# Record scatters of a graph kernel: eleven tiles per step beside the pair experts instead of eight, and none beside the slice attention

## The chip, the cores and the metric

The kernel runs on one core of a Trainium2 chip, in a single launch. The metric is the device time in microseconds (us), and the median of three runs stands for the kernel. TensorE is called PE here, VectorE DVE, ScalarE ACT, GpSimd POOL and SyncE SP; SPq and POOLq are the queues from which SP and POOL issue transfers.

## The reference

Four layers, each a graph network and a feed-forward block, over 3125 nodes of 256 values and a graph of 53125 edges (src, dst, a 64-value attribute and a type for each edge). Between the blocks stand a residual and a layer norm:

```
x = x + L0_gnn(ln(x), src, dst)              # batch norm and two GIN convolutions
x = x + L0_ffn(ln(x))                        # slice attention
x = x + L1_gnn(ln(x), src, dst)              # graph attention
x = x + L1_ffn(ln(x))                        # 8 experts, the best two for each node
x = x + L2_gnn(ln(x), src, dst, edge_attr)   # edge network: the only one that reads edge_attr
...                                          # one expert, relations, deep experts
```

The slice attention projects every node, takes a softmax over 64 slices for each of 8 heads, sums the nodes into slice tokens, lets the tokens attend to each other and gives the result back to the nodes. L1_ffn is, for the two experts that a node picks, `gelu((xn * g + b) @ W1 + b1) @ W2 + b2`, with hidden width 1024. L2_gnn needs for each edge its source node, destination node and attribute, and sums the messages by source node.

## The kernel before

Nodes lie in NT = 25 tiles of 128 rows, edges in ET = 416 tiles of 128. The stages of `build` run one after the other: constants, sort_slots (twice), place_edges, gin, slice_attention, graph_attention, expert_pair, edge_update, one_expert, relations, deep_experts. A stage ends with a barrier over all engines. Within a stage each engine has its own program, and they meet in semaphores.

**The records.** edge_update reads a table `rec2` in DRAM, in which the edges stand sorted by source. A record is 68 floats (272 bytes): 64 of the attribute, the other node's number, the row within the tile and two zeros. The table is filled earlier, from POOL, beside other stages: for each tile of 128 edges one indirect DMA ("scatter", L554) writes 128 records to the rows that m.record names. A group is SG = 8 tiles. For a group, SP loads the attributes (`load_group`, L532: 256 KB in pieces of 256 bytes), and POOL copies the two numbers beside them (L547, L549), waits for the load (`arrived`) and issues the scatters (`send_groups`); before a buffer is loaded again SP waits for its scatters (`sent`). The 52 groups are spread over three stages: PLACED = 8 beside place_edges, EARLY - PLACED = 12 beside the slice attention's first big loop, with two buffers in m.XN ("normed" in the profile), and 32 beside the loop of expert_pair, with four buffers in m.AF ("sums").

**The slice attention's loop** (L1104 to L1236) is written out for all 25 tiles, in five rounds of five. Per tile PE runs 4 matmuls of scores (L1193) and 2 for their bias (L1195), whose end is `scored`, 4 for the values (L1199), whose end is `fxed`, and, one tile later, 8 that sum the tokens (L1183; `summed`). DVE takes the maximum as soon as `scored` comes (L1223), subtracts it (L1226), and after ACT's Exp (L1161) sums and divides (L1230 to L1234). ACT copies the values out once `fxed` comes (L1163), keeps the weights (L1151) and stages the next tile (L1147). Each f32 matmul in the code is two in the profile, so the profile counts 18 matmuls and 18 weight loads per tile. POOL has nothing else to do in this stage than the records, and SP after its three first loads neither.

**The pair experts' loop** (L1924 to L2081) takes W = 32 steps of 256 rows, one expert's weights to each. It is a runtime loop whose body holds four steps (`pipeline`: each engine runs a prologue, then the loop, then the last steps written out). Per step PE turns the rows (L2007, 4 matmuls), runs the first layer of the next step (L2018, 32 matmuls, a signal `made` after every 4) and the second layer of this one (L2029, 32 matmuls, `done`). ACT runs 8 Gelus (L2045) on what `made` gives, DVE shapes the turned rows (L2063) and adds the bias (L2071). SP's queue holds, per step, in this order: rows four steps ahead (L1968), w1 of three ahead (1 MB, L1973), w2 of two ahead (1 MB, L1978; waits for `done`), the store (L1982; waits for DVE) and the record group four ahead (L532):

```
            def load_records(d, u, r):
                if not isinstance(d, int) or d >= RING:
                    sp.wait_ge(sent[u], r * (16 * SG))
                load_group(sp, a["edge_attr_64"], records, d + EARLY, u, arrived)

            pipeline(sp, R, (4, load_rows), (3, load_w1), (2, load_w2), (0, store), (4, load_records), total=W)
```

So four groups are loaded ahead of the loop, and from then on one for each step that PE, DVE and SP have finished. POOL's own program (`send_groups`) is written out.

Of the kernel before, what the change touches and what calls it, by code (L numbers as in the profile page):

```python
# [25 lines left out]
P = 128  # L26
# [6 lines left out]
ET = -(-E // P)  # L33
EA = 64
# [5 lines left out]
SG = 8  # L40
# [8 lines left out]
RING = 4  # L49
PLACED = 8  # L50
EARLY = 20
EPS = 1e-5
# [376 lines left out]
def place_edges(nc, m, attr):  # L429

    HALF = NP // 2
    R = SG
    with Stage(nc) as st:
# [31 lines left out]
        @block.gpsimd  # L465
        def _(pool):
            pool.wait_ge(m.rec_blanked, 16 * -(-WP // (BLANK // 4)))
            pool.wait_ge(m.rows_blanked, 16 * ((ROWS + 2 * P) // (P * 6)))
            send_groups(nc, pool, m, records, range(PLACED), arrived, sent, filled)

        @block.sync
        def _(sp):
            for g in range(PLACED):
                if g >= RING:
                    sp.wait_ge(sent[g % RING], g // RING * 16 * SG)
                load_group(sp, attr, records, g, g % RING, arrived)
            for u in range(RING):
                sp.wait_ge(sent[u], len(range(u, PLACED, RING)) * 16 * SG)
# [50 lines left out]

def load_group(sp, attr, records, g, u, arrived):  # L530

    sp.dma_start(records[:, u * SG:(u + 1) * SG, 0:EA], attr.rearrange("(t p) c -> p t c", p=P)[:, bass.ds(g * SG, SG), :]  # L532
                 ).then_inc(arrived[u], 16)


def send_groups(nc, pool, m, records, groups, arrived, sent, filled):

    RING = len(sent)

    nc.gpsimd.memset(records[:, :, EA + 2:EA + 4], 0.0).then_inc(filled, 1)  # L540
    pool.wait_ge(filled, 1)
    for n, g in enumerate(groups):
        u, r = n % RING, n // RING
        mine, group = slice(u * SG, (u + 1) * SG), slice(g * SG, (g + 1) * SG)
        if r:
            pool.wait_ge(sent[u], r * 16 * SG)
        nc.gpsimd.tensor_copy(records[:, mine, EA], m.oth_e[:, group]).then_inc(filled, 1)  # L547
        pool.wait_ge(filled, 2 * n + 2)
        nc.gpsimd.tensor_copy(records[:, mine, EA + 1], m.lo_e[:, group]).then_inc(filled, 1)  # L549
        pool.wait_ge(filled, 2 * n + 3)  # L550
        pool.wait_ge(arrived[u], r * 16 + 16)
        for k in range(SG):
            t = g * SG + k
            nc.gpsimd.indirect_dma_start(m.rec2, bass.IndirectOffsetOnAxis(ap=m.record[:, t:t + 1], axis=0),  # L554
                                         records[:, u * SG + k, :], None).then_inc(sent[u], 16)

# [464 lines left out]
def slice_attention(nc, m, a):  # L1021
# [84 lines left out]
    with Stage(nc) as st:  # L1106
        filled = st.sem("filled")
        arrived, sent = st.sems("arrived", 2), st.sems("sent", 2)
        records = view(xn, 5280, 2 * SG, EA + 4)
        names = ("loaded", "staged", "scored", "read", "centred", "expd", "weighted", "fxed", "fxcopied", "summed",  # L1110
# [10 lines left out]
        @block.sync  # L1121
        def _(sp):
            sp.dma_start(b_fx, a["L0_ffn_b_fx"].unsqueeze(0).to_broadcast([P, HW])).then_inc(loaded, 16)
            sp.dma_start(w_out, a["L0_ffn_W_out"].rearrange("(r p) d -> p r d", p=P)).then_inc(loaded, 16)
            sp.dma_start(b_out, a["L0_ffn_b_out"].unsqueeze(0).to_broadcast([P, D])).then_inc(loaded, 16)
            sp.wait_ge(loaded, 48)
            for n in range(EARLY - PLACED):
                if n >= 2:
                    sp.wait_ge(sent[n % 2], n // 2 * 16 * SG)
                load_group(sp, a["edge_attr_64"], records, PLACED + n, n % 2, arrived)  # L1130
            for u in range(2):
                sp.wait_ge(sent[u], (EARLY - PLACED) // 2 * 16 * SG)

        @block.gpsimd
        def _(pool):
            for s in range(U):
                ins = nc.gpsimd.memset(fx[:, s, :, FW - 1], 1.0)
            ins.then_inc(oned, 1)
            send_groups(nc, pool, m, records, range(PLACED, EARLY), arrived, sent, filled)

# [781 lines left out]
def expert_pair(nc, m, a):  # L1922
# [11 lines left out]
    with Stage(nc) as st:  # L1934
        names = ("turned", "shaped", "made", "active", "done", "ready", "smalls")
        turned, shaped, made, active, done, ready, smalls = (st.sem(s) for s in names)
        R = RING
        filled = st.sem("filled")
        arrived, sent = st.sems("arrived", RING), st.sems("sent", RING)
        records = view(m.AF, 0, RING * SG, EA + 4)  # L1940
        assert EARLY + W == ET // SG
        camex, came1, came2, stored = (st.sems(s, R) for s in ("camex", "came1", "came2", "stored"))
# [16 lines left out]
        def _(sp):  # L1959
# [24 lines left out]
            def load_records(d, u, r):  # L1984
                if not isinstance(d, int) or d >= RING:
                    sp.wait_ge(sent[u], r * (16 * SG))
                load_group(sp, a["edge_attr_64"], records, d + EARLY, u, arrived)

            pipeline(sp, R, (4, load_rows), (3, load_w1), (2, load_w2), (0, store), (4, load_records), total=W)
            for u in range(R):  # L1990
                sp.wait_ge(stored[u], 16 * (W // R + (1 if u > 1 else 0)))
                sp.wait_ge(sent[u], 16 * SG * (W // R))

        @block.gpsimd
        def _(pool):
            send_groups(nc, pool, m, records, range(EARLY, ET // SG), arrived, sent, filled)

# [1086 lines left out]
```

## Time and profile before

| what | value |
|---|---|
| median of three runs | 7234.84 us (7220.34 to 7235.94) |
| the profiled execution's own time | 7225.76 us |
| its span (first to last instruction) | 7224.1 us |
| busy: PE, PEld, DVE, ACT, POOL | 70%, 45%, 46%, 23%, 47% |
| mean granted TensorE clock | 0.819 |
| DMA packets from POOL's queue, share of 16 engines | 17.4% |

PE is the matmul side of TensorE and PEld its weight loads. Every time is from one profiled execution, counted from the span's start. In the order of time, an entry in square brackets is the idle time ahead of the instruction and what the profile takes for its end; "issue" is a wait for nothing that the profile shows, and a DMA named there can be one that merely came last. PEclk is the granted clock of TensorE as a share of full speed: 1.00 is 2.4 GHz, 0.50 is 1.2 GHz, and values between mix stretches of the two.

### The profile page before, as it was taken

The numbers are of one execution on the slowest core, as the hardware profiler recorded it, in microseconds if no ns is written. First come the engines' busy times: TensorE is split into PE (matmuls) and PEld (weight loads), VectorE is DVE, ScalarE is ACT, GpSimd is POOL, SyncE is SP. The second block draws the span as 40 slices with busy tenths as digits, with TensorE's granted clock in tenths as the row PEclk, the third lists the DMA queues.
The fourth block names the chain that finished last, engine by engine and source line by source line (L and its number), as shares of the span: only waits on it lengthen the run. The fifth ranks groups of instructions, "written<-read, shape, count | busy, mean of one in ns | idle before, by whom it ended". The sixth has DMA issues, their size and how long they took to land. (4 is left out here: it accounts for less than half of the span.)

```text
span 7224.1 us, 73624 instructions
## 1 busy us (share of the span) xinstructions
PE 5038.9 (70%) x20207; PEld 3266.0 (45%) x20208; DVE 3353.9 (46%) x7945; ACT 1675.0 (23%) x4060; POOL 3374.7 (47%) x3515
## 2 busy tenths in 40 slices
PE   5946766676638588867774499389998459576545
PEld 1214444444415233345553388378885234343334
DVE  5953334333515466666667011456665442343412
ACT  2930002000212367731112122133333111000111
POOL 4026772666250266657770555266660120666322
PEclk6968888777869689977777699699999779788877
DMA  4013332333110000023330577233340134333245
GB/s 178 2 54 91 91 91 58 89 91 91 32 48 1 22 2 2 2 70 90 91 90 9 160 220 213 69 101 103 106 99 16 52 96 146 90 91 91 51 144 170
DMA packets 405755, 597.99 MB, mean 83 GB/s; under 512 B 131359, under 2 KB 305759, under 8 KB 405279
## 3 DMA queue, kind: packets, MB, share of 16 engines
q0 software_dynamic: 144992, 337.62, 17.4%
q1 hardware_dynamic: 257200, 252.99, 11.3%
q8 instruction: 153, 2.51, 0.1%
q10 hardware_dynamic: 3216, 3.28, 0.1%
q14 instruction: 194, 1.59, 0.1%
HBM read 472.47 MB, written 121.17 MB: 82 GB/s over the span
## 5 line engine op out<-in xcount | busy, mean ns | idle before, releaser
L711 PE MATMUL ps<-zerow,zerob 128*128 128x440 bf16 x2640 | 812.3, 394 | 655.1 <-issue 399.4
L699 POOL DMA_INDIRECT wide<-table,src x880 | 882.0, 1002 | 792.7 <-ACTq L95 404.4
L741 DVE TENSOR_TENSOR sums<-sums,ps 128x256 f32 x1320 | 555.3, 421 | 1237.3 <-PE ps L714 490.4
L714 PE MATMUL ps<-wide 128*128 128x256 f32 x2640 | 906.8, 428 | 20.1 <-DMA wide<-table,src 7.9
L711 PEld LDWEIGHTS ps<-zerow,zerob 128*128 128x128 bf16 x2640 | 245.3, 104 | 999.7 <-issue 569.8
L714 PEld LDWEIGHTS ps<-wide 128*128 128x128 f32 x2640 | 568.8, 219 | 195.0 <-issue 60.6
L699 POOL DMA_INDIRECT wide<-table_rel,rel x440 | 437.8, 995 | 417.0 <-ACTq L95 218.5
L1642 POOL DMA_INDIRECT wide<-table_gat,src x440 | 472.5, 1074 | 218.4 <-issue 121.9
L2255 POOL DMA_INDIRECT work<-table,work x440 | 442.6, 1006 | 262.5 <-PE ps L2292 129.4
L1530 POOL DMA_INDIRECT work<-table_max,src x440 | 438.4, 996 | 198.9 <-issue 128.5
L1549 PE MATMUL ps<-wide,work 128*128 128x512 f32 x880 | 491.0, 642 | 0.0
L1673 PE MATMUL ps<-wide,work 128*128 128x260 f32 x880 | 323.9, 510 | 122.5 <-issue 62.5
L1511 ACT ACTIVATE wide<-ident,work 128x128 f32<-128x128 f32 x1320 | 397.9, 386 | 23.5 <-DMA work<-table_max,src 19.0
L649 ACT COPY work<-sums 128x256 f32<-128x256 f32 x100 | 31.7, 401 | 1359.7 <-PEq L653 1359.6
L660 PE MATMUL ps<-ident,work 128*128 128x128 f32 x650 | 112.2, 332 | 331.8 <-ACT work L649 331.8
L554 POOL DMA_INDIRECT rec<-sums,record x256 | 248.2, 970 | 200.4 <-DMA sums<-in_edge_attr 127.6
L1578 DVE TENSOR_REDUCE work<-ps 128x16 f32<-128x2048 f32 x110 | 251.8, 2290 | 190.9 <-DMA normed<-in_edge_attr 127.6
L2283 PE MATMUL ps<-wide 128*128 x880 | 272.1, 392 | 45.3 <-DVE work L2321 34.4
L1673 PEld LDWEIGHTS ps<-wide,work 128*128 128x128 f32 x880 | 190.8, 243 | 206.3 <-issue 139.3
L1547 PE MATMUL ps<-identb,work 128*128 128x512 bf16 x440 | 180.4, 410 | 148.6 <-issue 108.2
L521 PE MATMUL ps<-wide 128*128 128x441 f16 x832 | 229.1, 365 | 69.5 <-ACT wide L462 48.0
L1744 DVE TENSOR_TENSOR sums<-sums,ps 128x260 f32 x440 | 186.6, 424 | 175.9 <-DMA work<-table_max,src 97.3
(446 smaller groups left out, 9246.1 us busy)
## 6 DMA issues: line engine op xcount, KB each, us to landing
wide<-in_L_ffn_W SPq DMA_DIRECT2D x64, 1024.0 KB
wide<-in_L_ffn_expert_w SPq DMA_DIRECT2D x90, 256.0 KB
table_rel<-wide SPq DMA_DIRECT2D x20, 1024.0 KB
work<-rows_in SPq DMA_DIRECT2D x62, 256.0 KB
rows_out<-work SPq DMA_DIRECT2D x62, 256.0 KB
work<-rec SPq DMA_DIRECT2D x110, 136.0 KB
rec<-work SPq DMA_DIRECT2D x27, 544.0 KB, 16.4
wide<-table,src POOLq DMA_INDIRECT x880
```

Of the source, the lines that this page charges most:

```text
L699: nc.gpsimd.indirect_dma_start(rows[:, w % RT, :], None, table, bass.IndirectOffsetOnAxis(ap=index[:, w:w + 1], axis=0)).then_inc(gathered ...
L711: nc.tensor.matmul(m.PS[:, w % (2 * Q), 0:WT], m.zerob[:, 0:P], m.zerow[:, 0:WT], start=True, stop=True)
L714: nc.tensor.matmul(m.PS[:, w % (2 * Q), 0:D], S[:, w % RT, :], rows[:, w % RT, :], start=True, stop=True).then_inc(summed, 1)
L741: v.tensor_tensor(at, at, m.PS[:, s, 0:D], ALU.add).then_inc(added, 1)
L1511: nc.scalar.mul(diag[:, k * Q + s, h, :], m.ident[:], rows[:, u * Q + s, h:h + 1])
L1530: nc.gpsimd.indirect_dma_start(rows[:, q, :], None, m.table_max, bass.IndirectOffsetOnAxis(ap=m.src1[:, w:w + 1], axis=0)).then_inc(gather ...
L1549: mm = nc.tensor.matmul(at, S[:, k * Q + s, :], diag[:, k * Q + s].rearrange("p h e -> p (h e)"), start=False, stop=True)
L1578: v.reduce_max(top[:, half * Q:(half + 1) * Q, :], m.PS[:, half * Q:(half + 1) * Q, :].rearrange("p s (h e) -> p s h e", h=H), AX).then_in ...
L1642: nc.gpsimd.indirect_dma_start(rows[:, q, :], None, m.table_gat, bass.IndirectOffsetOnAxis(ap=m.src1[:, w:w + 1], axis=0)).then_inc(gather ...
L1673: te.matmul(m.PS[:, 4 + s, 0:RW], S[:, u * Q + s, :], rows[:, u * Q + s, :], start=True, stop=True).then_inc(summed, 1)
L2255: nc.gpsimd.indirect_dma_start(rows[:, k, 0:D], None, m.table, bass.IndirectOffsetOnAxis(ap=idx[:, u * Q + s:u * Q + s + 1], axis=0)).then ...
L2283: te.matmul(at, ST[:, k, :], tile_at(by_src, tiles[s]), start=True, stop=False)
```

## The change

The 12 groups beside the slice attention go; their 96 tiles are sent beside the pair experts, where a group grows from SG = 8 tiles to LG = (416 - 64)/32 = 11. The number of groups there stays 32, one per step, and so does the number of buffers, four. A load is 352 KB instead of 256 KB. `load_group` and `send_groups` take the first tile and the group's size as arguments; place_edges passes 8 and does what it did before.

```diff
 def slice_attention: the loop's stage
-        records = view(xn, 5280, 2 * SG, EA + 4)
             sp.wait_ge(loaded, 48)
-            for n in range(EARLY - PLACED):
-                if n >= 2:
-                    sp.wait_ge(sent[n % 2], n // 2 * 16 * SG)
-                load_group(sp, a["edge_attr_64"], records, PLACED + n, n % 2, arrived)
-            for u in range(2):
-                sp.wait_ge(sent[u], (EARLY - PLACED) // 2 * 16 * SG)
...
             ins.then_inc(oned, 1)
-            send_groups(nc, pool, m, records, range(PLACED, EARLY), arrived, sent, filled)
...
 def expert_pair
-        records = view(m.AF, 0, RING * SG, EA + 4)
-        assert EARLY + W == ET // SG
+        LG = (ET - PLACED * SG) // W
+        records = view(m.AF, 0, RING * LG, EA + 4)
+        assert PLACED * SG + W * LG == ET
...
             def load_records(d, u, r):
                 if not isinstance(d, int) or d >= RING:
-                    sp.wait_ge(sent[u], r * (16 * SG))
-                load_group(sp, a["edge_attr_64"], records, d + EARLY, u, arrived)
+                    sp.wait_ge(sent[u], r * (16 * LG))
+                load_group(sp, a["edge_attr_64"], records, d * LG + PLACED * SG, LG, u, arrived)
...
-                sp.wait_ge(sent[u], 16 * SG * (W // R))
+                sp.wait_ge(sent[u], 16 * LG * (W // R))
...
-            send_groups(nc, pool, m, records, range(EARLY, ET // SG), arrived, sent, filled)
+            send_groups(nc, pool, m, records, range(PLACED * SG, ET, LG), LG, arrived, sent, filled)
```

## Rows read from the trace of the kernel before

**Rows 1.** Line L554: count, min/median/max in ns, first and last start.
```profile
L554 POOL DMA_INDIRECT rec<-sums,record x256: 963/968/989, 4050.8 to 4505.0; - x128
L554 POOL DMA_INDIRECT rec<-normed,record x96: 963/968/1233, 2019.7 to 2148.5; - x96
L554 POOL DMA_INDIRECT rec<-work,record x64: 963/968/1187, 97.6 to 182.8; - x64
```
**Rows 2.** ACT in order of time: Exp starts, slice attention (start, us, engine).
```profile
2022.31 0.63 ACT L1161 ACTIVATE work<-work 128x512 f32<-128x512 f32 x1 [10.35 <-DVEq L1228]
...
2174.80 0.63 ACT L1161 ACTIVATE work<-work 128x512 f32<-128x512 f32 x1 [4.43 <-DVEq L1228]
...
2234.14 0.63 ACT L1161 ACTIVATE work<-work 128x512 f32<-128x512 f32 x1 [4.42 <-DVEq L1228]
...
2255.55 0.63 ACT L1161 ACTIVATE work<-work 128x512 f32<-128x512 f32 x1 [3.96 <-DVEq L1228]
```
**Rows 3.** Windows, slice attention: stretch, us, five engines busy (instructions), PEclk, DMA share, GB/s.
```profile
2040.00:2155.00 115.00, 33.90 (x81) 15.26 (x79) 12.96 (x24) 8.15 (x16) 82.42 (x101) 0.65 0.17 45
2174.80:2204.47 29.67, 28.20 (x91) 13.25 (x90) 15.96 (x30) 9.73 (x21) 0.00 (x0) 1.00 0.00 0
```
**Rows 4.** In order of time, slice attention: PE's two signals and their readers.
```profile
2040.95 1.12 PE L1195 MATMUL ps<-sums,ones 1*128 1x512 f32 x2
2042.00 1.98 PE L1199 MATMUL ps<-sums,work 128*128 128x512 f32 x4
...
2056.08 0.69 DVE L1223 TENSOR_REDUCE normed<-ps 128x8 f32<-128x512 f32 x1 [10.74 <-DMA wide<-table,src]
...
2061.75 0.59 ACT L1163 COPY work<-ps 128x512 f32<-128x512 f32 x1 [3.43 <-DMA wide<-table,src]
```
**Rows 5.** POOL in order of time: first scatter of a group, slice attention.
```profile
2052.42 0.98 POOL L554 DMA_INDIRECT rec<-normed,record  x1 [0.51 <-issue]
```
**Rows 6.** Windows of place_edges, beside scatters and after them.
```profile
120.00:180.00 60.00, 14.53 (x33) 2.17 (x32) 9.27 (x32) 10.64 (x16) 45.21 (x55) 0.50 0.14 39
205.00:225.00 20.00, 19.26 (x74) 4.69 (x74) 19.36 (x74) 20.00 (x37) 0.00 (x0) 1.00 0.01 1
```
**Rows 7.** Windows of the pair experts: the opening burst, the running loop.
```profile
4069.00:4096.00 27.00, 11.55 (x21) 5.41 (x20) 1.00 (x2) 1.68 (x4) 18.70 (x25) 0.59 0.36 116
...
4101.00:4500.00 399.00, 399.00 (x1905) 351.31 (x1904) 47.32 (x84) 93.76 (x230) 223.40 (x274) 1.00 0.73 221
```
**Rows 8.** DVE in order of time: two ends of a step, 27 steps apart.
```profile
4116.53 0.69 DVE L2071 TENSOR_TENSOR work<-ps,work 128x512 f32<-128x512 f32 x1 [12.07 <-PE ps L2029]
...
4501.35 0.69 DVE L2071 TENSOR_TENSOR work<-ps,work 128x512 f32<-128x512 f32 x1 [12.13 <-PE ps L2029]
```
**Rows 9.** POOL in order of time, pair experts: first and last scatter, next burst's first.
```profile
4239.37 0.98 POOL L554 DMA_INDIRECT rec<-sums,record  x1 [3.25 <-DMA sums<-in_edge_attr]
...
4248.29 0.97 POOL L554 DMA_INDIRECT rec<-sums,record  x1 [0.30 <-issue]
...
4253.83 0.98 POOL L554 DMA_INDIRECT rec<-sums,record  x1 [4.10 <-DMA sums<-in_edge_attr]
```
**Rows 10.** In order of time, same step: SP's queue and ACT's first instruction.
```profile
4246.39 0.01 SPq L1982 DMA_DIRECT2D rows_out<-work  x1
...
4247.82 0.01 SPq L532 DMA_DIRECT2D sums<-in_edge_attr  x1
...
4250.88 1.28 ACT L2045 ACT_TABLE_LOAD   x1 [11.08 <-PE ps L2018]
```
**Rows 11.** PE in order of time, opening of the pair experts.
```profile
4069.33 0.38 PE L2018 MATMUL ps<-work,wide 128*128 128x256 f32 x1 [0.29 <-issue]
...
4096.21 5.90 PE L2029 MATMUL ps<-wide 128*128 128x256 f32 x15 [0.82 <-issue]
```
**Rows 12.** DMA by queue, 2016 to 2155: packets, MB, share of 16 engines.
```profile
q8 instruction: 1, 0.02, 0.0%
q14 instruction: 1, 0.01, 0.0%
```

More of the change, by code:

```diff
@@ L50 @@
 PLACED = 8
-EARLY = 20
 EPS = 1e-5
@@ L468, in _ @@
             pool.wait_ge(m.rows_blanked, 16 * ((ROWS + 2 * P) // (P * 6)))
-            send_groups(nc, pool, m, records, range(PLACED), arrived, sent, filled)
+            send_groups(nc, pool, m, records, range(0, PLACED * SG, SG), SG, arrived, sent, filled)
         @block.sync
@@ L475, in _ @@
                     sp.wait_ge(sent[g % RING], g // RING * 16 * SG)
-                load_group(sp, attr, records, g, g % RING, arrived)
+                load_group(sp, attr, records, g * SG, SG, g % RING, arrived)
             for u in range(RING):
@@ L527, in _, with load_group, send_groups @@
             mm.then_inc(placed, 1)
[L530 to L536, printed above, removed]
+def load_group(sp, attr, records, first, size, u, arrived):
+    sp.dma_start(records[:, u * size:(u + 1) * size, 0:EA],
+                 attr.rearrange("(t p) c -> p t c", p=P)[:, bass.ds(first, size), :]).then_inc(arrived[u], 16)
+def send_groups(nc, pool, m, records, firsts, size, arrived, sent, filled):
     RING = len(sent)
@@ L541, in send_groups @@
     pool.wait_ge(filled, 1)
-    for n, g in enumerate(groups):
+    for n, first in enumerate(firsts):
         u, r = n % RING, n // RING
-        mine, group = slice(u * SG, (u + 1) * SG), slice(g * SG, (g + 1) * SG)
+        mine, group = slice(u * size, (u + 1) * size), slice(first, first + size)
         if r:
-            pool.wait_ge(sent[u], r * 16 * SG)
+            pool.wait_ge(sent[u], r * 16 * size)
         nc.gpsimd.tensor_copy(records[:, mine, EA], m.oth_e[:, group]).then_inc(filled, 1)
@@ L551, in send_groups @@
         pool.wait_ge(arrived[u], r * 16 + 16)
-        for k in range(SG):
-            t = g * SG + k
+        for k in range(size):
+            t = first + k
             nc.gpsimd.indirect_dma_start(m.rec2, bass.IndirectOffsetOnAxis(ap=m.record[:, t:t + 1], axis=0),
-                                         records[:, u * SG + k, :], None).then_inc(sent[u], 16)
+                                         records[:, u * size + k, :], None).then_inc(sent[u], 16)
 def blank_records(nc, pool, m, buf, blanked, stored):
@@ L1106, in slice_attention @@
     with Stage(nc) as st:
-        filled = st.sem("filled")
-        arrived, sent = st.sems("arrived", 2), st.sems("sent", 2)
-        records = view(xn, 5280, 2 * SG, EA + 4)
         names = ("loaded", "staged", "scored", "read", "centred", "expd", "weighted", "fxed", "fxcopied", "summed",
```

## The prediction

> **What bounds the kernel now.** I read the page first (no engine is busy for more than 70% of the span, so stages have to be read one by one), then the scatters by line, then the two stretches that the change touches, engine by engine in order of time, then both stretches in windows. The line view of L554 gives 416 scatters of 0.968 us: 64 in place_edges, 96 in the slice attention, 256 in the pair experts [rows 1]. The 96 run from 2019.7 to 2149.5.
>
> The slice attention's loop should be paced by DVE and ACT at one round of five tiles per 29.67 us: that is its pace once the scatters are over ((2234.14 - 2174.80)/2), with the granted clock at 1.00, the 2.4 GHz level [rows 2, 3]. The first Exp (L1161) starts at 2022.3; four rounds later, and 21.41 into the last one (2255.55 - 2234.14), would be 2162.4. The last Exp is at 2255.55 [rows 2]. While scatters run, PE gets 81 matmuls into 115 us, where it later gets 91 into 29.67, and its granted clock is 0.65 [rows 3]. No DMA is short: the DMA share is 0.17 there.
>
> What is late is PE's word. PE has run L1195 of one tile by 2042.1, and DVE, which waits for nothing else, reads that bank at 2056.1; PE ends L1199 at 2044.0 and ACT copies it at 2061.8 [rows 4]. The two lie 5.7 us apart, with 4 matmuls and 4 weight loads between them: 0.71 us per PE instruction. I call that choking. The breaks between groups of eight scatters do not lift it: two copies of 0.20 and a wait of 0.51, about 0.98 without a scatter [rows 5]; it goes on until the last scatter. place_edges shows the same: 33 matmuls in 60 us beside scatters, at the 1.2 GHz level, 74 in 20 us after them [rows 6].
>
> The pair experts' loop is bound by PE: 100% busy over 399 us at clock 1.00, 1905 matmuls and 1904 loads (9.55 instructions per us) [rows 7], and the step is (4501.35 - 4116.53)/27 = 14.25 us [rows 8]. Beside it POOL sends 8 scatters, 9.9 us from the first start (4239.37) to the last end (4249.26), then waits for SP's next load, and starts again at 4253.83: 4.6 us of rest [rows 9]. Choking is there too, late in each burst: SP's queue, which needs no PE for it, goes from its store to its record load in 1.43 us, and ACT gets the first signal of L2018, due about 4246.7, at 4250.9, 1.6 after the last scatter [rows 10]. It begins some 6.5 us into a burst and is lifted about 1.4 after it, and it costs nothing, because PE can run on with signals outstanding and the rest comes every step. In the stage's opening burst (32 scatters in a row from 4050.80, 42.5 us) it isn't hidden: PE stops at 4069.3, 18.5 us into it, does 21 matmuls in 27 us, and is free at 4096.2 [rows 1, 7, 11].
>
> **The change part by part.**
>
> Removed: 96 scatters, 24 POOL copies and 12 loads of 256 KB beside the slice attention. POOL's own time there is on no path; what comes back is the choking: 2255.55 - 2162.4 = **-93 us**. Bounds: -93 if all the lateness is the scatters', and -87 if what passes between the last scatter (2149.5) and DVE's next tile (some 6 us later) has another cause.
>
> Moved: the same 96 scatters to the pair experts, 11 in a group and 352 KB in a load. Copies and loads fall from 32+12 groups to 32 (24 POOL copies of 0.20 and 12 issues are saved, on no path). DMA: a group of eight with its load takes 0.17 of 10.87 us, so three more tiles take 0.7 us per step where the share is 0.73 [rows 3, 7]; not a bound.
>
> Opening burst: four groups of 11 are 4 x (11 x 1.273 + 0.69) - 0.98 = 57.8 us instead of 42.5, and the first, larger load lands about 1.5 later. PE is freed 17 us later and has done some 11 more matmul pairs by then (2.5 us of work): **+14 us**. Bounds 0 and +17.
>
> Steady loop: 11 scatters last 13.7 us; with copies and wait a group takes 14.69 us of POOL, over the step of 14.25. So POOL no longer rests by itself. If nothing choked, the step would be POOL's: 28 x 0.44 = +12 us, the lower bound. But a break of 0.98 doesn't lift the choking [rows 5]. I place PE's stop at 14.5 us into a burst: 9.9 us never stop it, 18.5 did, with some 65 instructions outstanding, and at 9.55 - 1.35 per us these are reached 8 us after the onset at 6.5. Then:
> - Two bursts in a row (28.4 us): PE stands from 14.5 to 29.8, 15.3 us, does 21 instructions (2.2 us of work) and loses 13.1. PE's "done" sits in the choke, so SP issues no further load until 29.8; its queue takes 1.5 and the landing 6 to 7 (4247.82 to 4253.83 is 6.0 for 256 KB [rows 9, 10]), so POOL starts again at about 38.
> - PE's step then ends about 6 us into the next burst, SP's load goes out already choked, lands 16.5 after the burst's start, and this burst stays single. Then the phase is early again and two join.
> - Three groups in 38 + 16.5 = 54.5 us by POOL; by PE 3 x 14.25 + 13.1 = 55.9, and up to 58.5 with the low clock after a stand (15 matmuls in 5.90 us [rows 11], 3.3 at full clock). That is 18.2 to 19.5 per step; I take 18.5: 28 x 4.25 = **+119 us**. Upper bound, if every pair of groups joins (38 us for two): 28 x 4.75 plus nine wakes of 2.6 = +156.
>
> Added waits: none new. SP's wait on sent[u] before a load stands ahead of its rows, w1, w2 and store; the group it asks for was loaded four turns earlier and is sent by then, since POOL has at most two groups before it.
>
> Sum: -93 + 14 + 119 = +40. On the profiled run's own 7225.76 that is 7266; the median of the runs is 9 above it. I take 7272, near the upper of the two (7275).
>
> **A rule beside the rows.** In the slice window the trace holds a single packet of the one instruction queue and one of the other [rows 12], and from 4200 to 4300 the answer lists none. The Trainium skill (Runtime: NRT & Kernel Launch, Instruction fetch mechanics) says that engines stream code in 16 KiB blocks over a DMA queue of their own, in sequence, and that only code outside the loaded window must be fetched. By it, written-out code could starve beside scatters while a loop that is loaded could not. That result is rival A. Against it stand SP and ACT, which are choked inside the loop in each burst [rows 10].
>
> **The rivals.**
>
> A, faster: the code supply of written-out stages is what scatters starve. Place: the slice attention and the opening of the experts, not the running loop. For it: all long stands (slice attention, place_edges, opening) are in written-out code or a loop's first pass. Then -93 + 14 + 12 = -67: 7168. It decides if PE is not stopped by bursts over 14.5 us within the loop. Chance 0.20.
>
> B, faster by less: choking as I say, but the system settles with every burst single, the landing late by its own choke, the break 2 us, step near 16: -93 + 14 + 28 x 1.75 = -30: 7205. For it: SP's lateness does postpone the load. Against it: PE's step end moves earlier in the burst each time that the load comes late. Chance 0.13.
>
> C, same: between B and mine, step near 17: -93 + 14 + 77 = -2: 7233. Chance 0.12.
>
> D, the moved work is hidden and the slice attention gains nothing (PE's signals late for another reason): 7234 + 26 = 7261. The end of the lateness with the last scatter speaks against it. Chance 0.03; it is within my range.
>
> Mine, slower, 0.52 (7272, its own range 7250 to 7320; past that, if most groups join).
>
> **How the numbers follow.** Slower by over 0.2% (which is about what a measurement of this kernel can tell): 0.55. Within it: 0.13. Faster: 0.32, A and B less their edges. The range reaches down to A with its bounds and up to the upper bound of the steady loop: 7158 to 7325.
>
> **What the profile after would show.** Exp's first to last in the slice attention 140 us (was 233), no L554 there, clock near 1. In the experts: 44 scatters in a row at the start, PE free 14 us later. In the loop: breaks of 0.98 between some bursts and over 8 us after others, PE busy 75 to 80% instead of 100, L2071's distance alternating between 14 and some 28 us. If it is regular at 14.7, A is right; at 16, B. I am wrong above all if 0.98 us of break is enough for a looping PE, or if PE's store of outstanding signals is larger than 65.

## The result and the profile after

The changed kernel takes 7319.22 us (median of 4 runs, 7308.93 to 7326.91), the kernel before 7231.72 in the runs beside it: a ratio of 1.0135, 95% interval [1.012, 1.015], slower by some 88 us between the medians, beyond doubt (the two medians alone give 1.0121; the ratio and its interval are taken over all runs). The forecast was 7272, slower by 40. The side was right and the size was not. The profiled execution has a span of 7325.1 us, 101 above that of before.

The slice attention did what was forecast. The time-ordered view of ACT, the Exp (now L1153), answering to [rows 2]:

```profile
2022.25 0.63 ACT L1153 ACTIVATE work<-work 128x512 f32<-128x512 f32 x1 [10.35 <-DVEq L1220]
...
2162.35 0.63 ACT L1153 ACTIVATE work<-work 128x512 f32<-128x512 f32 x1 [3.95 <-DVEq L1220]
```

First to last is 140.1 us where it was 233.2: -93. The windows answer to [rows 3] and [rows 7] (slice attention, opening burst, 28 steps of the pair experts; columns as there):

```profile
2040.00:2155.00 115.00, 109.12 (x347) 50.82 (x345) 61.35 (x115) 37.31 (x77) 0.00 (x0) 1.00 0.00 1
```

```profile
3975.00:4018.00 43.00, 11.74 (x26) 6.23 (x26) 0.99 (x2) 1.68 (x4) 30.84 (x37) 0.58 0.29 89
4025.51:4601.97 576.46, 478.22 (x1904) 375.73 (x1903) 47.34 (x85) 99.99 (x230) 309.20 (x362) 0.86 0.53 162
```

In the slice attention PE now gets 347 matmuls into the same 115 us that held 81. In the opening it does 26 matmuls in 43 us, and in the loop the same 1904 matmuls and 1903 loads that took 399 us at 100% busy take 576.5 at 83%, at a granted clock of 0.86 in place of 1.00. The DMA share falls (0.53): the transfers wait too.

A burst is a group's scatters, sent one after the other; a joined pair is two bursts with so short a break that PE stays held through the second. One joined pair, engine by engine. POOL first (answers to [rows 9]): first and last scatter of the pair's first burst, first and last of its second burst, then the first scatters of the next pair's two bursts.

```profile
4193.58 0.98 POOL L553 DMA_INDIRECT rec<-sums,record  x1 [13.81 <-DMA sums<-in_edge_attr]
...
4206.31 0.96 POOL L553 DMA_INDIRECT rec<-sums,record  x1 [0.30 <-issue]
...
4208.55 0.98 POOL L553 DMA_INDIRECT rec<-sums,record  x1 [0.80 <-DMA sums<-in_edge_attr]
...
4221.27 0.97 POOL L553 DMA_INDIRECT rec<-sums,record  x1 [0.30 <-issue]
...
4236.55 0.98 POOL L553 DMA_INDIRECT rec<-sums,record  x1 [13.83 <-DMA sums<-in_edge_attr]
...
4251.46 0.98 POOL L553 DMA_INDIRECT rec<-sums,record  x1 [0.74 <-issue]
```

PE in the same stretch (answers to [rows 11]):

```profile
4206.25 1.67 PE L2022 MATMUL ps<-wide 128*128 128x256 f32 x7
4208.52 0.38 PE L2022 MATMUL ps<-wide 128*128 128x256 f32 x1 [0.60 <-issue]
4209.99 0.38 PE L2022 MATMUL ps<-wide 128*128 128x256 f32 x1 [1.09 <-issue]
...
4221.38 0.59 PE L2022 MATMUL ps<-wide 128*128 128x256 f32 x1 [1.54 <-issue]
4223.47 3.90 PE L2022 MATMUL ps<-wide 128*128 128x256 f32 x7 [1.51 <-issue]
4227.17 0.85 PE L2000 MATMUL ps<-ident,work 128*128 128x128 f32 x4
```

DVE's end of a step (L2064; answers to [rows 8]), and SP's store and record load (answers to [rows 10]):

```profile
4025.51 0.69 DVE L2064 TENSOR_TENSOR work<-ps,work 128x512 f32<-128x512 f32 x1 [39.78 <-PE ps L2022]
...
4199.23 0.69 DVE L2064 TENSOR_TENSOR work<-ps,work 128x512 f32<-128x512 f32 x1 [14.05 <-PE ps L2022]
...
4227.54 0.69 DVE L2064 TENSOR_TENSOR work<-ps,work 128x512 f32<-128x512 f32 x1 [26.23 <-PE ps L2022]
...
4601.97 0.69 DVE L2064 TENSOR_TENSOR work<-ps,work 128x512 f32<-128x512 f32 x1 [24.20 <-PE ps L2022]
```

```profile
4202.07 0.01 SPq L531 DMA_DIRECT2D sums<-in_edge_attr  x1
...
4228.40 0.40 SPq L1975 DMA_DIRECT2D rows_out<-work  x1
4229.01 0.37 SPq L531 DMA_DIRECT2D sums<-in_edge_attr  x1
```

Read together: the step ends 5.65 us into the burst (4199.23). SP's load goes out at 4202.07 and is down by 4208.55, 15.0 us into the burst, so the second burst follows almost at once. PE works without a break up to 4207.92 (14.3 us in) and comes free at 4223.47, 29.9 us in, after a stand of 15.6 in which it starts 18 matmuls (32 take 7.07 us at full pace). Up to there it is the forecast. But at that moment PE still owes the step 7 matmuls, and they take 3.90 us, since the granted clock is 0.50 there (the 1.2 GHz level). Only at 4227.54 does DVE get its bank, SP loads at 4229.01, and POOL starts at 4236.55, 43.0 us after the pair's start. The step ends 5.5 us into this burst as well, and the next pair joins too. From 4190 to 4240 the DMA view lists no packet of either instruction queue.

### The profile page after: what moved, and what is told of

Same layout as the page of the kernel before. It is cut to its first block and busy times, and to the rows that moved or that the text cites. A ratio compares the mean times of both kernels' runs of the same rounds, so it can differ in the third digit from the quotient of the medians.

```text
span 7325.1 us, 73574 instructions
## 1 busy us (share of the span) xinstructions
PE 5117.0 (70%) x20207; PEld 3287.4 (45%) x20208; DVE 3356.8 (46%) x7945; ACT 1681.2 (23%) x4060; POOL 3362.6 (46%) x3490
## 5 line engine op out<-in xcount | busy, mean ns | idle before, releaser
L713 PE MATMUL ps<-wide 128*128 128x256 f32 x2640 | 909.2, 429 | 20.2 <-DMA wide<-table,src 8.4
L713 PEld LDWEIGHTS ps<-wide 128*128 128x128 f32 x2640 | 570.4, 219 | 195.3 <-issue 62.7
L553 POOL DMA_INDIRECT rec<-sums,record x352 | 340.5, 967 | 294.6 <-DMA sums<-in_edge_attr 185.9
L2022 PE MATMUL ps<-wide 128*128 128x256 f32 x1024 | 295.8, 423 | 114.1 <-issue 111.4
L2022 PEld LDWEIGHTS ps<-wide 128*128 128x128 f32 x1024 | 209.4, 209 | 190.3 <-issue 165.8
L2064 DVE TENSOR_TENSOR work<-ps,work 128x512 f32<-128x512 f32 x32 | 22.1, 692 | 583.3 <-PE ps L2022 457.4
```

The costliest lines, as they stand in the source:

```text
L713: nc.tensor.matmul(m.PS[:, w % (2 * Q), 0:D], S[:, w % RT, :], rows[:, w % RT, :], start=True, stop=True).then_inc(summed, 1)
L2022: mm = te.matmul(m.PS[:, 6 + u % 2, s * D:(s + 1) * D], hid[u % 2][:, j, s * P:(s + 1) * P], w2[u % 2][:, j, :], start=(j == 0), stop=(j = ...
```

## The experiments

They were taken in seven sittings, each on one chip with its own runs of the kernel before. The times of before did not agree. Four of them, on four different chips, gave 7151, 7223, 7170 and 7230 us (the time of before was 7232 where the prediction was made). Three gave 6601, 6599 and 6600. I call the two kinds **with the delay** and **without it**; only the ratio within a sitting is used.

**Parts alone, with the delay (before 7151.47).** The kernel before with the 96 left out of the slice attention (their records stay blank: this part of the computation is missing):

```
-            for n in range(EARLY - PLACED):
-                ...
-                load_group(sp, a["edge_attr_64"], records, PLACED + n, n % 2, arrived)
-            send_groups(nc, pool, m, records, range(PLACED, EARLY), arrived, sent, filled)
```

> The kernel before with the 12 groups beside the slice attention left out (96 tiles of records are never written); the pair experts keep 8 per step. Theory (unbroken scatters choke PE's signals): the slice attention's loop gets back 93 us, the experts are as before: 7232 - 93 = 7139, step 14.25 us. Rival (PE's signals are late in the slice attention for another reason): 7232. Rival (the loss after is an effect of the shorter slice attention on later stages): 7139 plus some of the 196 lost.

Measured: 7080.05, ratio 0.9903 [0.9876, 0.9931], -71 us. Exp's first to last is 140.1 us. The windows of the slice attention and of 28 steps:

```profile
2015.00:2130.00 115.00, 109.12 (x347) 51.07 (x346) 61.86 (x118) 37.62 (x78) 0.00 (x0) 1.00 0.00 1
3962.71:4361.68 398.97, 398.97 (x1906) 351.31 (x1905) 47.34 (x85) 94.34 (x230) 224.13 (x275) 1.00 0.73 221
```

The stage gives back all that was forecast and the loop stays at 14.25. That the total falls by 71 and not 93 is not explained by this stage; before itself spread from 7131 to 7172 in this sitting, and no trace of it was taken there. Other stages do vary: those that gather rows (three aggregations, two loops of the graph attention, edge_update's first loop) take 4050 us together in the first trace of before and 3992 in this one, each counted from its first instruction to the next stage's.

The other part: the changed kernel with the slice attention's 96 sent as before, too (they are then sent twice).

```
+            for n in range(12):
+                ...
+                load_group(sp, a["edge_attr_64"], records, (PLACED + n) * SG, SG, n % 2, arrived)
+            send_groups(nc, pool, m, records, range(PLACED * SG, 20 * SG, SG), SG, arrived, sent, filled)
```

> The changed kernel with the 12 groups beside the slice attention put back as well (their 96 tiles are sent twice). Theory: the two halves are independent, so 7319 + 93 = 7412, experts' step 20.6 us as in the changed kernel. Rival (the experts suffer from coming earlier, or from what the slice attention leaves behind): under 7380.

Measured: 7343.8, ratio 1.0273 [1.0244, 1.0302], +192 us: 232.9 us in the slice attention, the opening 66.1 (before 51.6), and

```profile
4083.18:4626.22 543.04, 462.15 (x1906) 372.28 (x1905) 47.34 (x85) 98.97 (x230) 303.56 (x355) 0.89 0.58 173
```

19.4 us per step. The profiled spans of these two kernels differ by 259.5 us, of which 92.8 lie in the slice attention, 16.2 in the opening and 144.0 in the loop. So the loss is made in the pair experts by eleven per step, and the gain in the slice attention is separate from it.

**Load or scatters, same sitting.** The changed kernel that loads 11 tiles and sends 8 of them (three tiles' records per group are missing):

```
-        for k in range(size):
+        for k in range(sends):
```

> The changed kernel, loading 11 tiles per step (352 KB) but scattering only the first 8 of them (96 tiles of records are never written). Theory: bursts of 8 with rest, step 14.25: 7139, as e1, plus at most 3 us for the first load's later landing. Rival (the larger loads collide with the weights or land late): much of the 196 us stays, 7250 to 7319.

Measured: 7084.18, ratio 0.9904 [0.9878, 0.993]; the loop's window:

```profile
3966.53:4365.49 398.96, 398.96 (x1905) 351.30 (x1905) 47.34 (x85) 95.33 (x230) 223.93 (x274) 1.00 0.77 228
```

14.25 us per step at a DMA share of 0.77. The larger load costs nothing; the three more scatters cost everything.

**The break between bursts, same sitting.** The changed kernel with two POOL memsets ahead of each group of 11:

```
+        for scratch in rest:
+            nc.gpsimd.memset(scratch, 0.0).then_inc(filled, 1)
+            f += 1
+            pool.wait_ge(filled, f)
...
+                        rest=[m.WS[:, 5300:7100]] * 2)
```

> The changed kernel, and in the pair experts POOL fills scratch columns twice (about 3.9 us in all) ahead of each group of 11: more POOL work, but no two bursts join. Theory: rest of 4.9 us lifts the choke each time, the step is POOL's 13.7 + 0.98 + 3.9 = 18.6 us, so 28 x (18.6 - 20.6) = -56, and the opening burst, now in four parts, gives back some 30 of the 43 us it costs: 7319 - 86 = 7233. Rival (POOL's time or the volume of scatters per step sets the pace): nothing is gained, 7319 or later, up to 28 x 4.6 more if rests add to the cycle (7448).

Measured: 7169.24, ratio 1.0027 [1.0013, 1.0041]. No burst joined another; the break is 4.3 us, a group takes POOL 18.0, the opening is 31.7 us (66.1 in the kernel with both parts, same sitting), and 28 steps take 460.2 us: 16.43 on average, from 9.5 to 22.3 one by one, where 18.6 was expected. POOL ends 572 us after it began: it, not PE, now sets the stage's end.

With one memset, in a later sitting with the delay (before 7230.39):

> The changed kernel with one POOL memset of 1800 columns ahead of each group of 11, a break of 2.6 us in place of 0.98 (4.3 with two memsets gave single bursts, PE's steps at POOL's pace of 18, ratio 1.0027). Where signals are delayed: if 2.6 us lifts the delay, no stand of PE in the loop, steps at POOL's 16.3 us, opening near +32, ratio 0.990 to 0.997; if it does not, bursts act as one row, PE stands for 10 us and more in pairs, step 19 or over, ratio 1.01 or more.

Measured: 7179.5, ratio **0.9932** [0.9916, 0.9949]. POOL around a break, and the loop's window:

```profile
4101.11 0.97 POOL L560 DMA_INDIRECT rec<-sums,record  x1 [0.30 <-issue]
4102.08 1.62 POOL L546 MEMSET work<- 128x1800 f32 x1
...
4104.73 0.99 POOL L560 DMA_INDIRECT rec<-sums,record  x1 [0.51 <-POOL sums L554]
```

```profile
3989.88:4441.35 451.47, 414.01 (x1897) 347.01 (x1896) 47.36 (x85) 94.83 (x230) 349.99 (x385) 1.00 0.67 207
```

A break of 2.65 us (4102.08 to 4104.73) in place of 0.98 lifts the delay before the next burst: nearly every step is 16.2 to 16.5 us, which is POOL's own time for a group (4104.73 to 4121.11), and PE's clock is 1.00. Slowing POOL by 1.7 us per group turned a ratio of 1.0135 into one of 0.9932.

But the delay still acts late in every burst, and it is what holds PE to POOL's pace here. PE around the same break:

```profile
4097.87 3.62 PE L2019 MATMUL ps<-work,wide 128*128 128x256 f32 x16
4102.66 1.11 PE L2019 MATMUL ps<-work,wide 128*128 128x256 f32 x4 [1.17 <-issue]
4104.10 2.85 PE L2019 MATMUL ps<-work,wide 128*128 128x256 f32 x12 [0.34 <-issue]
```

It pauses at 4101.49, 13.1 us into the burst (first scatter 4088.35), and does 4 matmuls in 2.6 us. The same kernel in a sitting without the delay has the same breaks, 16.35 us per group too, and its first 17 steps take 14.25 us each, with PE busy throughout:

```profile
3618.46:3860.71 242.25, 242.25 (x1158) 213.31 (x1157) 28.74 (x52) 61.84 (x140) 187.90 (x208) 1.00 0.75 224
```

That the time of the break counts, and not the memset in it, is shown by breaks that came about by themselves, while POOL waited for a load. In the loops of the changed kernel, of the one with both parts and of the 16-byte one below, 13 breaks of 2.27 to 3.84 us lie between bursts of 11, four of them (2.78 to 3.12) in the changed kernel: PE starts 18 to 21 matmuls from 1 to 5 us into the next burst and as many from 5 to 9, its full pace. After the 30 breaks of 0.98 to 1.79 us it starts 4 to 10 and 2 to 9. Of five in between, four (1.87 to 2.03) give full pace for the first 4 us and 6 to 9 matmuls in the next, and one (2.09) full pace in both, but 10 matmuls from 9 to 13 us in.

**Bytes or rows, with the delay (before 7170.17).** The changed kernel with rows of 16 bytes in place of 272, to a table of their own (the pair experts' share of the records stays blank):

```
-            nc.gpsimd.indirect_dma_start(m.rec2, ...,
-                                         records[:, u * size + k, :], None)
+            nc.gpsimd.indirect_dma_start(m.narrow if narrow else m.rec2, ...,
+                                         records[:, u * size + k, 0:4 if narrow else EA + 4], None)
```

> The changed kernel with each record row of the pair experts cut to 16 bytes and sent to a table of its own (records of those tiles are blank downstream, which by itself cost 50 us in later stages where there was no delay). Under the delay: if the bytes written are what delays TensorE's signals, the step falls from 20.6 to 14.3 to 14.7 us; if it is the count of rows or of scatters, the loop stays at 19 to 21 us per step. Without the delay: 14.25 again.

Measured: 7275.16 (two runs), ratio 1.0148 [1.0118, 1.0177]; a scatter still takes POOL 0.97 us, and

```profile
3980.70:4548.28 567.58, 474.91 (x1906) 375.39 (x1905) 47.34 (x85) 100.23 (x230) 310.45 (x362) 0.87 0.51 148
```

20.3 us per step. Seventeen times fewer bytes change nothing, so what delays TensorE's signals is not the bytes written. Sixteen and 272 bytes were the only two sizes tried, and the number of rows (128) was not.

**No long row of scatters anywhere.** The kernel before with its 96 spread: 24 go to place_edges, 72 stay beside the slice attention but in threes, and place_edges' own are parted after every fourth; the first groups of the pair experts are parted by memsets.

```
-PLACED = 8
+PLACED = 11
...
+                        pace=lambda i: pool.wait_ge(stepped, i * 4) if i and i % 4 == 0 else None)
...
+        if rest is not None and 0 < n < RING:
+            for k in range(2):
+                nc.gpsimd.memset(rest, 0.0).then_inc(filled, 1)
...
+                        pace=lambda i: pool.wait_ge(kept, U + i // 3) if i and i % 3 == 0 else None)
```

> As for the spread kernel before, on whichever chip it lands: on one that delays TensorE's signals, 0.980 to 0.990 if the unbroken run does it, and no gain beyond 0.995 if the mean rate of scatters does; on one that does not, 1.000.

Measured (before 7222.93): 7066.56, ratio **0.9782** [0.9765, 0.9798], -156 us; no version that does the whole work was faster with the delay (the next one is level). It is a little beyond the 0.980 to 0.990 expected. Its windows (place_edges, slice attention, the pair experts' 28 steps):

```profile
120.00:180.00 60.00, 57.88 (x218) 13.97 (x218) 58.48 (x220) 60.00 (x109) 28.71 (x36) 1.00 0.11 30
1960.00:2075.00 115.00, 108.95 (x347) 51.08 (x346) 62.28 (x116) 37.00 (x76) 59.26 (x74) 1.00 0.13 34
3908.86:4333.80 424.94, 406.91 (x1905) 353.71 (x1905) 47.32 (x85) 94.57 (x230) 245.13 (x299) 0.97 0.70 209
```

72 scatters beside the slice attention leave its pace at 140.3 us, first to last Exp. PE's 218 matmuls in place_edges stood at 33 [rows 6]. Scatters as such don't delay PE, rows of them do. The gain lies in these two stages: place_edges takes 238.7 us where it took 306.7, though it has 24 scatters more, and the slice attention gives 92.9. The experts gave nothing (496.7 us for the stage, 496.6 before): their opening is 26.1 us (51.6 before), but two steps took 21.1 and 33.3 us, because four groups ran as one row of 32: groups 3 to 6, counted from 0 as the code does, and only group 3 has memsets ahead. I tried to cure that with memsets ahead of groups 1 to 7:

> The spread kernel with the two POOL memsets ahead of groups 1 to 7 of the pair experts in place of 1 to 3. In the spread kernel groups 4 to 7 joined into a row of 32 scatters and the steps beside it took 21.1 and 33.3 us (+26 us). Where signals are delayed: if the unbroken row did it, all 28 steps take 14.25 us and the ratio to before falls from 0.978 to some 0.974 to 0.976; if not, the two long steps stay. Where they are not: 1.000.

Measured (before 7230.39): 7068.51, ratio 0.9778 [0.9761, 0.9794]; 28 steps 425.5 us. That expectation missed (it counts the groups from 1): the row of 32 moved to groups 7 to 10, and two steps took 22.7 and 32.4. Both times the four loads lay ready when the memsets ended, and POOL sent them all at once.

**Sittings without the delay.** The changed kernel itself (before 6599.4):

> The changed kernel itself, beside the three others, to see on this chip what its ratio is. If the chip delays TensorE's signals beside scatters as in the traces of before and after: ratio 1.012 to 1.025, pairs of bursts, some 20.6 us per step. If it is a chip without the delay (before near 6600): the slice gains nothing (its loop is at full pace already), and POOL alone paces the pair experts: 28 x 0.44 = +12 us and the last scatter some 20 to 60 us later, so a ratio of 1.002 to 1.012; steps regular at 14.3 to 14.7.

Measured: 6614.35, ratio 1.0019 [1.0009, 1.0029]. Windows (place_edges, slice attention, 28 steps) and line L553:

```profile
120.00:180.00 60.00, 57.84 (x218) 13.83 (x216) 58.62 (x218) 60.00 (x110) 45.38 (x55) 1.00 0.14 39
1800.00:1915.00 115.00, 109.12 (x347) 50.94 (x346) 61.18 (x116) 37.02 (x76) 0.00 (x0) 1.00 0.00 0
3617.17:4016.14 398.97, 398.97 (x1906) 351.31 (x1905) 47.35 (x85) 101.15 (x230) 300.43 (x356) 1.00 0.80 235
```

```profile
L553 POOL DMA_INDIRECT rec<-sums,record x352: 963/967/987, 3590.4 to 4058.2; - x176
```

POOL is as busy in place_edges as in [rows 6] (55 instructions, 45 us) and PE does 218 matmuls, not 33. In the experts all 352 scatters form one row, with no break over 0.98, and PE never stands. What is left of the change is POOL's own pace: 14.7 us per group, so it ends 8 us after PE's last step (4059.1 against 4051.1), and the kernel is 0.2% slower.

The others without the delay. Ten per step, with four groups left in the slice attention (before 6601.43):

> Ten tiles per step beside the pair experts and four groups of eight (instead of none or twelve) beside the slice attention. A group of ten is a burst of 12.4 us and a POOL cycle of 13.4, under the step of 14.25, so that POOL rests 1.8 us per step by itself. Theory: 1.8 us is about what it takes until PE's signals are through (choke seen up to 1.5 to 2.0 after a burst), so some bursts join: step between 14.3 and 18; slice attention 30 us over its 140. Against before: -63 there, +11 for the opening burst of 40, and 0 to +105 in the loop. Rival (the step is POOL's cycle or PE's, whichever is longer): step 14.25, -52.

Measured: 6600.68, ratio 1.000 [0.999, 1.001]: 14.25 us per step with 260 scatters in a row. Ten per step was never run with the delay, so its expectation on joining bursts is untested. The one memset ahead of each group of 11, twice:

> As e3_rest_between with one fill of scratch instead of two: breaks of 2.6 us between bursts of 11 instead of 4.3. Theory: if 2.6 us lifts the choke, POOL's 32 x 16.35 = 523 us bound the stage, 55 less than with two fills, so some 35 us below the kernel before on the same chip. If 2.6 isn't enough, pairs join and it is near the changed kernel, 1.3% over before. Rival (rests only help because they slow POOL down): later than with two fills or the same.

> The changed kernel with one POOL memset of 1800 columns ahead of each group of 11, which makes the break between bursts some 2.6 us in place of 0.98. On a chip that delays: if the rest has to outlast the 1.4 us that the lifting takes, 2.6 is enough, every burst is single, and the step is POOL's, 16.3 us: slice -93, opening +8 or so over before, loop 28 x 2.1 = +59, some 0.99 to 1.00; if 2.6 does not lift it, pairs join and the ratio is 1.01 or more. On a chip without the delay: POOL-bound, 1.010 as before.

Measured: 6667.74, ratio 1.0103 [1.0086, 1.012], and 6663.52, 1.0099 [1.0081, 1.0118]: POOL takes 16.35 us per group and ends the stage. Against the changed kernel, the break that gains 2% with the delay costs 0.8% without it. The 16-byte rows, three times:

> The changed kernel with the scatters beside the pair experts writing 16 bytes per row (4 of the 68 floats, to a table of their own; rec2 stays blank there): same count of scatters and rows, 1/17 of the bytes. Theory as far as it goes: it is the count of scatters without a break that chokes, step near 20, 1.3% over before. Rival (the bytes written or read choke): bursts don't choke, step 14.7 (POOL's), -93 + 12 + the opening: about 1% under before.

> The changed kernel with each record row of the pair experts cut to 16 bytes and sent to a table of its own, so the records of those tiles are blank downstream. Scatters stay at 11 per step and 128 rows each. On a chip that delays: if the bytes written are what delays TensorE's signals, the step falls from 20.6 to 14.3 to 14.7 us and the ratio to some 0.993; if it is the count of rows or of scatters, the loop stays at 19 to 21 us per step and the ratio at 1.01 to 1.02. On a chip without the delay both say what the changed kernel itself shows.

> The changed kernel with each record row of the pair experts cut to 16 bytes and sent to a table of its own, so the records of those tiles are blank downstream (which by itself cost 50 us in later stages on the chip without the delay). Scatters stay at 11 per step and 128 rows each. On a chip that delays: if the bytes written are what delays TensorE's signals, the step falls from 20.6 to 14.3 to 14.7 us; if it is the count of rows or of scatters, the loop stays at 19 to 21 us per step. On a chip without the delay: 14.25 again.

Measured: ratios 1.0104, 1.0092 [1.0074, 1.011] and 1.0096, with 14.25 us per step; the 50 us over the changed kernel appear in edge_update's first loop, which reads blank records (708.1 us against 655.7). In the run with the delay that loop took 710.8 us, no more than the changed kernel's 715.5, so nothing has to be taken off its ratio. The spread kernel, three times:

> A version after the theory, built on the kernel before: 11 groups in place_edges, 4 scatters and then a wait until ACT is 16 tiles on; 9 groups beside the slice attention, 3 scatters for each tile of nodes kept; 32 groups of 8 beside the experts as before, with two fills of scratch ahead of groups 1 to 3 to break the opening burst. Theory: place_edges gives back about 50 of the 60 us that its choke costs, the slice attention about 85 of 93, the opening 20: some 150 us or 2.1% under before. Rival (short bursts choke the chains that turn on every signal just as well): within 1% of before.

> No burst over 8 scatters anywhere: the 96 are spread (24 more paced in place_edges by ACT's steps, 72 beside the slice attention in threes per kept tile, and the opening groups of the experts are parted by two POOL memsets). On a chip that delays: if it is the unbroken run that does it, slice near 140 to 150 us (-85), place_edges about 15 to 25 us shorter for its 64 and longer for the 24 more, opening -15, loop 14.25, so a ratio of 0.980 to 0.990; if it is the mean rate of scatters or anything else, no gain beyond 0.995. On a chip without the delay: 1.000.

> No burst over 8 scatters anywhere: the 96 are spread (24 more paced in place_edges by ACT's steps, 72 beside the slice attention in threes per kept tile, and the opening groups of the pair experts are parted by two POOL memsets). On a chip that delays: if it is the unbroken run that does it, the slice's first to last Exp near 140 to 150 us (-85), opening near +30 in place of +51, loop 14.25, a ratio of 0.980 to 0.990; if it is the mean rate of scatters or anything else, no gain beyond 0.995. On a chip without the delay: 1.000 again.

Measured: 1.0007 [0.9997, 1.0016], 1.0005 [0.9995, 1.0015] and 1.0005 [0.9995, 1.0015]. With nothing to lift, spreading is worth nothing.

## Why the prediction was right in its side and wrong in its size

**Slice attention, -93: right.** The trace after has -93.1, the stage alone had it too, and the experts' first scatter comes at 3957.4, 93.4 earlier.

**Opening burst, +14: right.** First scatter to the end of the first step grew from 51.6 to 68.1, +16.5, inside the bounds of 0 to +17, and the row of 44 lasted 57.7 us where 57.8 was forecast. That it is the row's length is shown by the versions that part it: 31.7 and 32.5 us with 11 in a group and a break between groups.

**Steady loop, +119: this is the term that failed.** It measured 576.5 - 399.0 = +177.5, above even the upper bound of +156. The mechanism was right; the failed step is the first bullet of the steady loop: "SP issues no further load until 29.8; its queue takes 1.5 and the landing 6 to 7 [...], so POOL starts again at about 38." The stand was sized rightly (stop at 14.5 forecast, 14.3 measured; free at 29.8 forecast, 29.9 measured). But it was taken that PE's "done" was only held back. It had not been earned: 5.65 us into the burst the step had just begun, 8.7 us of its 14.25 were done when PE stopped, and after the stand PE still had 7 matmuls to do, 3.90 us at the low clock. The load goes out 35.4 us after the start and POOL starts at 43.0, not 38. In the eight cycles of a pair alone the step ended 31.7 to 34.6 us after the pair's start, and POOL started again 8.9 to 10.1 us later, where the forecast had 29.8 and some 8: most of the 5 us is the work still owed, about 1 the queue and the landing. Within the stand PE did more than forecast (18 matmuls and their loads, not 21 instructions).

The 28 steps consist of four cycles of a pair and a single burst (57.7 to 60.8 us for three steps, measured on the three that another follows) and eight of a pair alone (40.7 to 43.8 us for two). The forecast had only the first kind, at 3 x 18.5 = 55.5. With 43.0 in place of 38 in its own sum it is 43.0 + 16.5 = 59.5, or 19.8 per step: +156, which is 37 of the 58 us that were missing. The other 21 come from the second bullet, "lands 16.5 after the burst's start, and this burst stays single": at 4208.55 the load was down after 15.0, and eight times of twelve the next burst joined, at 21.2 us per step. The other four times it started 16.5 to 16.8 us after the last one's start, and the burst stayed single, as forecast. The upper bound held that case, but priced it at POOL's 38 us for two, although the forecast's own PE count was 28.5 + 13.1 = 41.6; taken from the larger, it would have been 28 x (41.6/2 - 14.25) = +183 and held the measured value.

**End and sum.** -93 + 16.5 + 177.5 + 2.4 (from the last of the 28 steps to the stage's end) = +103; the spans differ by 101.

**Luck and small slips.** The total, 7319.22, lies within the range of 7158 to 7325, and even just within mine of 7250 to 7320, although the loop's term lies above its bound and most groups did join. That is luck: the medians differ by 88 us where the profiled spans differ by 101, and the profiled run itself took 7326.91. The ends of the range do not follow from the stated bounds: -93 + 0 + 12 gives 7154 and -87 + 17 + 156 gives 7321. 7266 and 9 are 7275, not 7272. The onset at 6.5 us and the lifting after 1.4 stand in no row: [rows 10] shows SP late at 7.0 us into a burst and ACT served 1.6 after its last scatter. That PE stops because some 65 instructions are outstanding was worked out from such estimates; the stop itself came as forecast, and no run tested the reason.

**The rivals.** A, that the running loop cannot be starved, is refuted: PE stands for 15 us within it, again and again. The Trainium skill (Runtime: NRT & Kernel Launch, Instruction fetch mechanics), from which its mechanism came, describes how code arrives; the trace disagrees only with the use that A made of it, since looping and written-out stages stand alike, and the two instruction queues moved 7 packets in the 576 us of the changed loop. B, every burst single at 16 us per step, did not happen by itself, but it is near what a break of 2.65 us makes (16.35 per step, ratio 0.9932). C did not happen. D is refuted by the slice attention's 140.1. The number that A gave for its loop, 28 x 0.44 = +12, is near what the total shows without the delay (+13 by the ratio of 1.0019, with an interval of +6 to +19), but not where A put it: the 28 steps took 398.97 us, as before, and the time lies at the stage's end, where POOL's last scatters come after PE's last step.

**"0.98 of break doesn't lift it"** held: 0.98 does not, 2.65 does. Between them nothing was tried on purpose; the breaks that came about by themselves put the change between 1.79 us, where bursts still acted as one, and 2.27.

## What to carry to other kernels

Where POOL sends scatters one after another beside a PE-bound stage, look at how long a row runs without a break before counting POOL's idle time as free: eleven in a row that join into 22 cost 12 to 15 us per pair here (40.7 to 43.8 us for two steps in place of 28.5), eight with a rest cost nothing. Spread such work in small parts tied to a semaphore of the stage it runs beside, or put some other POOL work between the groups, which costs POOL's time where there is no delay (0.8% here). When a stall in a loop is priced, follow the loop until its phase repeats, and ask what the stalled engine still owes when it is freed: that remainder, here 3.9 us, comes before the signal that the next load waits for. And take both kernels in one sitting: the time of the same kernel differed by up to 9.6% between sittings (6599 to 7232), where the change was worth 1.35%.

## What the runs showed of the hardware that was not expected

The delay of TensorE's signals beside a row of indirect scatters is not always there. With the kernel before and its data the same, three sittings out of seven had none of it and ran at 6600 us in place of 7151 to 7230. One and the same chip was in both kinds of sitting, at 7151 and at 6600. Without it PE keeps its full pace beside 352 scatters in a row; with it PE starts 18 matmuls in the 15.6 us from 14.3 us into a row on, single ones 1.5 to 2.1 us apart (4208.52 to 4209.99, 4221.38 to 4223.47). What makes the difference stays open: the profiles of the changed kernel in either kind have the same packets and bytes in every DMA queue and the same 0.97 us per scatter, and no run here could vary it. The cause of the delay itself is open as well. Shown, for scatters, is what it hangs on: not the bytes written (16 or 272 per row), not the size of the loads, not the mean rate (eight per 14.25 us cost nothing, eleven per 20.6 us, a little fewer, cost 6.3 us of every step), but the length of the row and the break that follows.

The scatters are the smaller part of what it costs. The two traces of the changed kernel, with the delay and without, differ by 718 us. Of these 210 lie in the pair experts and 68 in place_edges, but 443 lie in the stages that gather rows with indirect DMAs from POOL: 250 in the three aggregations (1974 us against 1724), 133 in the graph attention and 60 in edge_update. The spread kernel leaves these stages as they are, and so it ends at 7067 and not near 6600. No run changed the gathers, so whether the same delay holds them, and whether breaks would help there, is not shown.

The Trainium skill (GPSIMD Engine Reference, When to use GPSIMD) says that DMAs which POOL issues have their descriptors made by a pair of its cores, one for the reads and one for the writes. That does not say what the cost of a scatter goes with; in the traces its issue takes 0.97 us at 16 and at 272 bytes per row, with 128 rows in both, and no run here shows what these cores do to another engine's signals.

Of the versions tried, the spread kernel does best over both kinds: it is 2.2% faster with the delay and, at 0.05% off, not measurably slower without it. The changed kernel loses in both, 1.35% and 0.2%.
